# Decoder layer on one core: softmax divided after the mix, two more joins, a packed last FFN tile, D·h written by ScalarE, new instruction orders

## What is computed

```python
x = _layernorm(x + attn(x))            # a Mamba block: scan over the sequence
x = _layernorm(x + xattn(x, ctx, ctx)) # attention, 16 heads of width 8
x = _layernorm(x + ffn(x))             # top 2 of 8 experts, and a shared one
# Mamba: conv, delta = softplus(...), and for each of 16 states n
new = dA * state + d_t * B_t * h_t;  y = sum_n(new * C_t) + D * h_t;  out = (y * gate) @ out_w
# attention
attn = softmax(scores);  out = attn @ v
# FFN: 9 experts of 176 rows each (1584 rows)
y = sum_e cw[e] * (silu(x @ wg[e]) * (x @ wu[e])) @ wd[e]
```

## Time and profile before

| | us |
|---|---|
| median of 3 runs | 1911.16 (1908.84 to 1911.6) |
| the profiled execution, its own time | 1910.89 |
| its span, first to last instruction | 1909.1 |
| start of `u<-delta,h` in the first and last chunk | 41.4 and 1663.7 |
| last `yg` (end of the last scan) | 1789.8 |

### The profile page before, as it was taken

One profiled execution on the slowest core, in us unless ns is written; L12 is line 12 of the kernel. 1 busy time (PEld: TensorE's weight loads), 2 busy tenths in 40 slices (PEclk: granted clock), 3 DMA queues, 4 the chain that ended last, 5 costly groups with the idle time before them and its releaser, 6 DMA issues. The chain is left out here.

```text
span 1909.1 us, 25699 instructions
## 1 busy us (share of the span) xinstructions
PE 1684.5 (88%) x7035; PEld 964.7 (51%) x7138; DVE 1539.7 (81%) x1891; ACT 1398.8 (73%) x4370; POOL 1529.5 (80%) x1284
## 2 busy tenths in 40 slices
PE   3679989999898999999899899989989999998976
PEld 1235454655545465554646455464645546465544
DVE  4988988888888888889888888888888888878422
ACT  5478787786977768787777869777787977867361
POOL 0578888888888888888888898888889888898734
PEclk7789999999999999999999999999999999999988
DMA  3212221313222131222213122221312222121102
GB/s 103 80 47 73 88 75 61 95 40 96 82 84 78 52 91 54 89 75 96 81 52 92 53 90 82 89 79 52 90 55 89 76 82 83 66 85 55 63 7 66
DMA packets 125918, 140.50 MB, mean 74 GB/s; under 512 B 44048, under 2 KB 69456, under 8 KB 125776
## 3 DMA queue, kind: packets, MB, share of 16 engines
q1 hardware_dynamic: 125776, 138.86, 23.8%
HBM read 133.84 MB, written 4.98 MB: 73 GB/s over the span
## 5 line engine op out<-in xcount | busy, mean ns | idle before, releaser
L1149 POOL TENSOR_TENSOR prod<-state,c_rep 128x1024 f32<-128x1024 f32 x256 | 605.4, 2368 | 39.8 <-PE p_y L627 23.7
L1018 DVE TENSOR_TENSOR_SCAN state<-decay,p_drive 128x1024 f32<-128x1024 f32 x256 | 584.6, 2284 | 28.5 <-ACT decay L766 15.2
L627 PE MATMUL p_y<-prod,ident 128*128 128x512 f32 x768 | 391.4, 609 | 10.2 <-POOL prod L1149 5.7
L766 ACT ACTIVATE decay<-delta,a_neg 128x504 f32<-128x504 f32 x512 | 359.3, 725 | 43.4 <-DVE state L1018 42.0
L1008 DVE TENSOR_TENSOR p_drive<-u,p_drive 128x1024 f32<-128x1024 f32 x256 | 312.2, 1220 | 66.4 <-PE p_drive L609 36.2
L898 ACT ACTIVATE ex<-p_ring,nmax 128x64 f32<-128x64 f32 x1024 | 310.1, 369 | 19.8 <-DVE nmax L1068 19.4
L898 ACT ACTIVATION_READ_ACCUMULATOR ex<-p_ring,nmax 128x1 f32 x1024 | 255.4, 262 | 0.0
L728 PE MATMUL p_ring<-x2T,wg 128*128 128x512 f32 x416 | 226.8, 650 | 13.2 <-ACT gh L823 12.3
L1202 POOL TENSOR_TENSOR ex<-ex,rden 128x512 f32<-128x512 f32 x128 | 144.2, 1127 | 94.1 <-DVE rden L1072 94.1
L728 PE MATMUL p_ring<-x2T,wu 128*128 128x512 f32 x416 | 208.9, 603 | 7.5 <-DVE km L1118 6.5
L627 PEld LDWEIGHTS p_y<-prod,ident 128*128 128x128 f32 x768 | 139.6, 194 | 143.8 <-issue 116.9
(11 more groups left out here) (139 smaller groups left out, 3080.1 us busy)
## 6 DMA issues: line engine op xcount, KB each, us to landing
c_rep<-c_rows SPq DMA_DIRECT2D x256, 256.0 KB, 3.6
cwr<-cw_rows SPq DMA_DIRECT2D x64, 256.0 KB, 3.2
ctxT<-in_ctx_t SPq DMA_DIRECT2D x32, 256.0 KB, 5.6
cwr<-cw_rows SPq DMA_DIRECT2D x32, 224.0 KB, 3.1
cwr<-cw_rows SPq DMA_DIRECT2D x32, 192.0 KB, 2.7
cwr<-cw_rows SPq DMA_DIRECT2D x32, 160.0 KB, 2.9
xf<-in_x SPq DMA_DIRECT2D x16, 256.0 KB, 5.9
xb<-in_x SPq DMA_DIRECT2D x16, 256.0 KB, 4.8
```

The source lines that it names most:

```text
L627: pe.matmul(p_y[1 - first][:], ident[:], prod[:, slot_of(c, n), 1 - first, :], start=False, stop=n == STATE - 1).then_inc(prod_used.sem, 1)
L766: act.activation(decay[:, n % 2, j, :].rearrange("p (b t) -> p b t", t=SEQ)[:, :, 1:], delta[:, c.parity, j, :].rearrange("p (b t) -> p b ...
L1018: dve.tensor_tensor_scan(state[:, slot_of(c, n), :, :].rearrange("p j t -> p (j t)"), decay[:, n % 2, :, :].rearrange("p j t -> p (j t)"), ...
L1149: pool.tensor_tensor(mine, state[:, slot_of(c, n), :, :], c_rep[:, n % C_SLOTS, :].unsqueeze(1).to_broadcast([128, HALVES, T]), ALU.mult). ...
```

## The change

1. **Softmax.** `scale` on POOL is gone. `ex` is transposed and mixed undivided. The row sums of 8 sequences are kept, and twice per chunk (after sequences 3 and 7) DVE takes the reciprocal of 32 values (`sum`), ACT spreads them over 8 columns per head into the buffer of `kT` (`spread`, 2 instructions), PE multiplies that by an identity, which transposes it (`rden`, 4 products of 128 columns), and DVE multiplies `aT` by the result (`share`, 2 instructions of 64 x 256). `aout` waits for `share`.
2. **Joins.** `JOINED` goes from 4 states to 6 (3 and 7 are new): two additions more on POOL, four `y_sum` fewer on PE (20 for 24).
3. **Last tile.** Tile 12 of the FFN has 48 rows (`REST`). The 48 up columns now stand at column 64 of the gate tile, so that one product `up_g12` makes both. ACT copies the up part to `us`, and POOL multiplies (`gu12`, new); `up_u12` and its multiplication on DVE are gone, and `down` takes 48 rows of that tile.
4. **D times h.** `y_d` moves from PE to ACT, which writes it into `p_y`; the first `y_sum` of each half waits for it, and it waits for `gated` of the chunk before.
5. **Orders.** All tables are new, for each engine and part.

```diff
-JOINED = (1, 9, 11, 13)
+JOINED = (1, 3, 7, 9, 11, 13)
-ON_POOL = (1, 2, 4, 5, 7, 8, 10)
+ON_POOL = (1, 2, 4, 5, 7, 8, 10, 12)
+REST = FFN_ROWS - 128 * (FFN_TILES - 1)
+SPLIT = FFN_TILES - 1
+UP_AT = 64
 ORDER_TEXT = {
     "pe": (
-        "scan.B_row1 front.hid0 tail.up_u9 tail.up_g11 tail.up_u10 tail.up_g12 back.y_sum30 "
+        "tail.up_g8 scan.B_row0 tail.up_u7 tail.up_g9 tail.up_u8 front.xnT0 tail.up_u9 tail.up_g10 "
...
+        spread = kT[:].rearrange("p (b c) -> p b c", c=128)
...
-                pe.matmul(p_y[j][:], diag_d[:, j, :], h[:, c.parity, j, :], start=True, stop=False)
...
+                if sum_index(k) < HALVES:
+                    pe.wait_ge(skip_ready.sem, skip_ready.at(c.m, first))
...
                 elif name == "turn":
-                    pe.wait_ge(scale_ready.sem, scale_ready.at(c.m, i))
+                    emptied(pe, "score", i, c.m)
...
+                elif name == "rden":
+                    pe.wait_ge(spread_ready.sem, spread_ready.at(c.m, i))
+                    for b in range(SIDE):
+                        mm = pe.matmul(p[:, b * 128:(b + 1) * 128], spread[:, b, :], ident[:], start=True, stop=True)
                 elif name == "aout":
-                    emptied(pe, "mix", (i + 1) * CHUNK_B // 2 - 1, c.m)
+                    emptied(pe, "rden", i, c.m)
...
+                elif name == "spread":
+                    act.wait_ge(rden_ready.sem, rden_ready.at(c.m, i))
...
+                    for s in range(2):
+                        a = act.activation(spread[:, :, 64 * s:64 * s + 64].rearrange("p b (a d) -> p b a d", d=HEAD_D),
+                                           mine, ACT.Copy)
...
+                elif name == "y_d":
+                    j = 1 - i
+                    act.wait_ge(h_ready.sem, h_ready.at(c.m, j))
+                    if c.m >= 1:
+                        act.wait_ge(yg_ready.sem, yg_ready.at(c.m - 1, i))
...
+                    act.activation(p_y[j][:], h[:, par, j, :], ACT.Copy, scale=column(V_D + j)
+                                   ).then_inc(skip_ready.sem, 1)
...
                 elif name == "sum":
-                    emptied(dve, "score", i, c.m)
-                    dve.reciprocal(rden[:, i % 2, :], den[:, i % 2, :]).then_inc(rden_ready.sem, 1)
+                    mine = slice(SIDE * i, SIDE * i + SIDE)
+                    emptied(dve, "score", SIDE * i + SIDE - 1, c.m)
...
+                    dve.reciprocal(rden[:, mine, :].rearrange("p b a -> p (b a)"),
+                                   den[:, mine, :].rearrange("p b a -> p (b a)")).then_inc(rden_ready.sem, 1)
+                elif name == "share":
+                    p = filled(dve, "rden", i, c.m)
+                    emptied(dve, "mix", SIDE * i + SIDE - 1, c.m)
...
+                        d = dve.tensor_tensor(a3, a3, p[r, :].rearrange("p (b s q) -> p b s q", b=SIDE, s=2)[:, :, s, :],
+                                              ALU.mult)
...
-                elif name == "scale":
...
-                    pool.tensor_tensor(ex[:, i % 2, :, :], ex[:, i % 2, :, :],
-                                       by_group(rden[:, i % 2, :]).to_broadcast([128, PAIRS, SEQ]),
-                                       ALU.mult).then_inc(scale_ready.sem, 1)
```

143 lines of the change are left out of this document (106 added, 37 removed), and 283 rows, old and new, of tables (FIRST_TEXT, LAST_TEXT, ORDER_TEXT).

## The result

The kernel after takes 1963.4 us, median of 4 runs (1958.0 to 1973.5), where before takes 1911.4: ratio 1.028, 95% interval 1.0249 to 1.0311. Forecast were 1864 us, range 1833 to 1900. It is slower by 52 us where I expected 47 less. The profiled execution took 1973.45 us (span 1971.7), the slowest of the four, so its trace shows some 10 us more than the median.

The account below looks back on a forecast made before the run. PE was taken as the fullest engine, bounding the FFN stretch, with no engine alone bounding attention. Terms of −2.7 and −0.6 us gave −3.3 a turn, over 14 turns −46.2, plus −1: 1910.9 − 47.2 = 1864 us, range 1833 to 1900.

Parts of the forecast that it names:

- four fifths of PE's 3.36: Attention stretch: of the 3.36 us a turn that PE loses there, 2.7 were to come out of the turn.
- 0.6 of 0.86: FFN stretch, PE 94% busy and taken as the bound: of 0.86 us saved by dropping `up_u12`, 0.6 a turn comes out.
- The prices: Times per instruction taken from before's trace, such as `share` 0.42 us, `spread` 0.474, a D write 0.68, a copy 0.59.
- I cost at nothing: FFN `down` with 48 rows of a tile instead of 128: 0 us, as a product streams the same 128 columns.
- I price the hops against each other at nothing: Attention stretch: the hop over DVE and POOL goes, one over DVE, ACT, PE and DVE comes, net 0 us.
- D writes at 0, up to 2.3 if they wait: `y_d` on ACT, waiting for `gated0`: falls into ACT's idle time, 0 us; without that cover up to a scan, 2.3.
- Rival D: Emptier stretches make PE's clock fall once more each turn: +20 to +25 us, forecast 1886; no chance of its own.
- Rival C: Slower: the loop over POOL and ACT gets longer, +2.7 us a turn, 1940 us in the middle; chance 0.10.
- 1.9 + 0.85 − 1.3: Attention stretch set by ACT: `spread` adds 1.9 us and `share` 0.85, against a scale and a reciprocal less, 1.3.
- Rivals A and B: A: PE alone bounds, 1851 or 1836 us, chance 0.19. B: DVE and scans bound, 1887 to 1904, chance 0.19.
- The port rule: DVE instructions with two SBUF inputs and GpSimd's SBUF reads exclude each other; 2.2 us a turn either way, left out.

Follow-up runs that it names:

- e5: Kernel before with four sums per chunk (products of states 2 and 6 in y) left out of TensorE, output incomplete: 1907.5 us, ratio 1.000.
- e6: Kernel before with six joins on GpSimd for four, and the four sums they make needless out of TensorE's order: 1950.0 us, ratio 1.023.
- e7: Kernel before with only the softmax edit, divided behind the mix, its eight scales gone from GpSimd: 2016.6 us, ratio 1.058.
- e14: Kernel after with four joins in place of six, the four sums back on TensorE: 1975.0 us, ratio 1.034 to before.
- e10: Kernel before with GpSimd's gate-weight products of FFN tiles 4 and 5 cut to 4 of 512 columns, output incomplete: 1889.6 us, ratio 0.991.
- e8: Kernel before with the packed last FFN tile alone: 1934.3 us, ratio 1.015.
- e3: Kernel after with `down` taking all 128 rows of the packed tile again: 1962.4 us, ratio 1.028 to before.
- e2: Kernel after with the second tanh on ScalarE moved back to its later place, behind the second turn: 1962.2 us, ratio 1.028 to before.
- e9: Kernel before with D times h alone moved from TensorE to two writes of ScalarE: 1954.9 us, ratio 1.025.
- e15: Kernel after with D times h back on TensorE, behind the query's product, none on ScalarE: 1945.3 us, ratio 1.017 to before.
- e11: Kernel after with TensorE products that nobody reads, behind the second transposition of x2 alone: 1947.6 us, ratio 1.021 to before.
- e16: Kernel after with four joins in place of six and D times h back on TensorE: 1957.7 us, ratio 1.025 to before.

## Why the prediction was wrong

**What bounds.** The step that failed is the one from busy shares to time: "four fifths of PE's 3.36" out of the attention stretch, −2.7 us, and 0.6 of 0.86 out of the FFN stretch, because "there PE is the bound". Measured were +2.1 and +1.8 us. In the attention stretch of before, TensorE's relief is worth nothing (e5), and the joins (e6) and the softmax (e7) that pay for it lengthen the path. In after's own orders the sums do cost time when they are put back (e14), so what a sum is worth depends on where it stands and not on how full its engine is; yet the stretch as a whole got longer there too. In the FFN stretch TensorE is not shown to be the wrong engine: 6.8 us at half rate, some 3.4 us of its work, made the stretch 3.3 us longer. GpSimd's run counts there as well (e10). What failed there is the clock, put at nothing in the sum.

**The prices** held. After has `share` at 413 ns (0.42), `spread` at 410 (0.474), a D write at 689 (0.68), the copy of the packed tile at 596 (0.59):

```profile
L1118 DVE TENSOR_TENSOR aT<-aT,p_ring 64x256 f32<-64x256 f32 x64 | 26.4, 413 | 14.1 <-PE p_ring L714 13.4 <-ACT aT L934 0.2
...
L927 ACT ACTIVATE kT<-rden 128x256 f32<-128x256 f32 x64 | 23.0, 410 | 0.4
L986 ACT ACTIVATE p_y<-h,vecs 128x512 f32<-128x512 f32 x32 | 21.9, 689 | 0.0
...
L968 ACT ACTIVATE us<-p_ring 48x512 f32<-48x512 f32 x16 | 9.5, 596 | 22.6 <-PE p_ring L731 19.7 <-POOL acts_more L1264 2.8
```

So did the loads: 96.4, 96.8, 93.0, 90.9 forecast for TensorE, VectorE, GpSimd, ScalarE; 99.3, 97.4, 94.5, 90.2 in the turn of 0.98. (The 0.98 turn is the rare one; in the usual turn PE is busy 105.1 us.) Right sizes, and a wrong sum: they were weighed by where engines are full, not by who is waited for.

**48 rows "I cost at nothing"**: wrong by 0.39 us a group, four groups a turn, 1.6 us on TensorE. In the orders of before they are most of what the packed tile cost in the FFN stretch (e8: 0.8 of 1.3 us); in after they are 0.9 of it (e3), which did not show in the median.

**"I price the hops against each other at nothing"**: alone, the dearest of the edits. The path over `sum`, `spread`, `rden` and `share` cost 6.8 us a turn in the orders of before; I had added its pieces and left out that each stands in a queue. In after's orders no run takes the softmax back, so its share there is open.

**D writes at 0, up to 2.3 if they wait**: `y_d` did not wait (0.0 us idle before it), and the edit still cost 47 us alone and 18 in after. The larger part of the price lay on TensorE, where the products it took away had been cover for the clock.

**Rival D, the clock**, happened, and larger: I had it "in the range, not a case of its own" with one fall a turn of 1.8 us, 20 to 25 us in all. Half rate grew by 10.5 us a turn; by the 0.30 us for each found over the runs of after and e2, an estimate is 3.1 of the 3.8 us that the turn grew. But without it there is no gain either. The first turn of after with only the short fall took 111.4 us (1069.8 to 1181.2); before's turns without a fall took 110.2 to 111.3, those with one of 3.4 us 111.6 to 112.5. So at the clock of before the change would be worth about nothing, and not my 47 us. (The other such turn is the last of the twelve; it took 111.3 us, and before's last 107.4.) The remaining ten turns are 4 to 6 us longer. The Trainium skill, "TensorE: Matmul & The Clock Gate", section "Part 1: The HAM clock gate (the "warmup" mystery)", has the throttled state as the default and activity as what lifts it; e9, e15 and e11 agree, each with its half rate.

**Rival C**, a loop that the edits make longer, got 0.10, and in part it is what the single edits show: the softmax cost 6.8 us where I had put 1.9 + 0.85 − 1.3, and the joins, which it left out, 2.5. Its `gu12` is not borne out: behind the last `cw10` the packed tile costs 0.8 of its 1.3 us (e8). Nor was ScalarE busy over 95% of after's attention stretch (48.7 of 53.6 us, 91%). At full clock the FFN stretch of after takes 59.4 us, no more than before's. **Rivals A and B** would both have needed TensorE's relief to pass through; it didn't.

**The port rule.** VectorE's taps in after, then in before:

```profile
L1071 DVE SCALAR_TENSOR_TENSOR zc<-hpad,halfv,zc 128x512 f32<-128x512 f32 x96 | 130.2, 1357 | 5.3 <-ACT zc L819 4.0
```
```profile
L1037 DVE SCALAR_TENSOR_TENSOR zc<-hpad,halfv,zc 128x512 f32<-128x512 f32 x96 | 101.4, 1056 | 3.6 <-ACT zc L812 2.3
```

With the same work that is 1.8 us a turn of longer instructions. Of the 96, 53 took over 0.9 us and all but one of these began inside an instruction of GpSimd; in before it was 26, all of them. So the orders brought more of them beside GpSimd's products. I left this out of the sum, and what it cost of the turn no run here separates.

**Still open**: why the clock of e9 also fell 7 us ahead of the key mask; how after's 2.1 us in the attention stretch divide (at most 1.1 for the clock by e11, 0.7 for the D product with its share of the clock by e15; joins, softmax and orders are not separated there); where the 46 us of e16 lie; and e14's 2.8 us, where TensorE's sums, worth nothing when taken out of before, cost 2.8 of the 3.4 us that they take when put into after.

## What to carry to other kernels

A product on a nearly full engine can be worth less than nothing to remove, if it filled a wait of that engine: look first at what the engine does just before and behind it. Follow the path back through one turn and price an edit by whose queue it stands in there, and test the main term with a kernel that leaves that work out before building on it. And when TensorE gets emptier, count the clock as a case of its own, with the time at half rate read from the trace.
